# Attention head loop: bias and mask added by identity matmuls in PSUM, and 1/z folded into the transposes of the probabilities

## What is computed

```python
scores = jnp.einsum('bhqd,bhkd->bhqk', q, k) / math.sqrt(HEAD_DIM)
masked = jnp.where(causal[None, None], scores, NEG)
chunk_max = padded.reshape(b, N_HEADS, s, n_chunks, CHUNK).max(axis=-1)
_, topk_idx = jax.lax.top_k(chunk_max, k_top)            # 8 chunks of 16 keys
allowed = causal & (tok_mask | init_mask | recent_mask)  # first 128, last 128 keys too
attn = jax.nn.softmax(jnp.where(allowed, scores, NEG), axis=-1)
out = jnp.einsum('bhqk,bhkd->bhqd', attn, v)
```

## Time and profile before

| | us |
|---|---|
| runs of the kernel before: median (2 runs, 6246.68 to 6270.27) | 6258.47 |
| profiled execution, device time | 6245.39 |
| its span on the slowest core (core 6) | 6243.7 |
| spans of the other cores | 6157.7 to 6235.6 |
| attention stage on core 6, from 1736 to about 4305 | 2569 |

### The profile page before, as it was taken

One profiled execution on the slowest core, in us unless ns is written; L12 is line 12 of the kernel. 1 busy time (PEld: TensorE's weight loads), 2 busy tenths in 40 slices (PEclk: granted clock), 3 DMA queues, 4 the chain that ended last, 5 costly groups with the idle time before them and its releaser, 6 DMA issues.

```text
span 6243.7 us, 55986 instructions; the slowest of 8 cores (6157.7 to 6243.7 us)
## 1 busy us (share of the span) xinstructions
PE 3077.5 (49%) x14003; PEld 1404.8 (22%) x14240; DVE 2022.3 (32%) x4597; ACT 1060.7 (17%) x2316; POOL 762.6 (12%) x1444
## 2 busy tenths in 40 slices
PE   5657665656612233444455555566777511275300
PEld 2222222222201121222222232333333211132100
DVE  1120002121165555555555454452000132211233
ACT  0000000000012232333333333442000022100011
POOL 3323332323300000000000000000222100121000
PEclk9879988888855555555555555556888855587655
DMA  8879996877800000000000000003777633473333
GB/s 135 123 104 138 134 137 100 121 106 113 119 1 7 7 1 8 1 7 1 7 1 1 8 1 7 1 1 78 169 170 166 145 121 121 118 162 64 83 116 114
DMA packets 408685, 471.05 MB, mean 75 GB/s; under 512 B 168064, under 2 KB 284800, under 8 KB 404032
## 3 DMA queue, kind: packets, MB, share of 16 engines
q0 software_dynamic: 207360, 252.27, 28.1%
q1 hardware_dynamic: 201024, 215.19, 11.0%
...
## 4 chain that ended last, share of the span: by engine, by line
DVE 27%; DMA 22%; PE 21%; issue 13%; ACT 11%; SPq 2%; DVEq 2%; another core or an unknown queue 1%; POOL 1%; ACTq 0%; POOLq 0%; PEldq 0%
DMA wqt<-wqT 6%; PE pw L502 5%; ACT Ebuf L445 5%; PE pq L238 4%; DVE Cm L383 3%; DMA wkvt<-wkT 3%; ACT Ebuf L452 3%; PE pk L160 3%; PE psS L434 3%; DMA wot<-woT 3%; DMA wkvt<-wvT 2%; DVE SBc L387 2%; DVE Cm L394 2%; DVE Pn L463 2%; PE pB L778 2%
## 5 line engine op out<-in xcount | busy, mean ns | idle before, releaser
L238 PE MATMUL pq<-xot,wqt 128*128 128x512 bf16 x2008 | 513.5, 404 | 198.3 <-DMA wqt<-wqT 154.9
L160 PE MATMUL pk<-xbt,wkvt 128*128 128x512 bf16 x2006 | 499.2, 394 | 196.4 <-DMA wkvt<-wkT 78.7
L318 PE MATMUL ptr<-identb,Pn 128*128 128x128 bf16 x2304 | 286.3, 307 | 625.8 <-DVE Pn L463 625.8
L502 PE MATMUL pw<-oft,wot 128*128 128x512 bf16 x2007 | 471.4, 390 | 168.3 <-DMA oft<-oscr 135.8
L493 POOL DMA_DIRECT2D wot<-woT x256 | 135.7, 530 | 3101.0 <-ACTq L97 2610.8
L333 PE MATMUL pso<-PT,Vtm 128*128 128x128 bf16 x2304 | 338.4, 265 | 254.2 <-ACT PT L324 105.7
L370 PE MATMUL psS<-Kfm,Qfm 128*128 128x512 bf16 (+1 forms) x624 | 317.7, 555 | 195.0 <-ACT Ebuf L445 188.5
L324 ACT COPY PT<-ptr 128x1024 bf16<-128x1024 bf16 (+3 forms) x384 | 294.6, 802 | 659.8 <-PE ptr L318 659.8
L318 PEld LDWEIGHTS ptr<-identb,Pn 128*128 128x128 bf16 x2304 | 225.5, 139 | 762.8 <-issue 762.8
L445 ACT ACTIVATE Ebuf<-psS,ngm 128x512 bf16<-128x512 f32 (+2 forms) x512 | 301.2, 588 | 308.9 <-PE psS L434 246.7
L452 ACT ACTIVATE Ebuf<-SBf,ngm 128x384 bf16<-128x384 f32 (+1 forms) x256 | 154.5, 604 | 1024.1 <-DVE SBf L421 1003.4
...
## 6 DMA issues: line engine op xcount, KB each, us to landing
xot<-xoT POOLq DMA_DIRECT2D x256, 256.0 KB, 5.6
oft<-oscr SPq DMA_DIRECT2D x256, 256.0 KB, 4.4
xbt<-xbT POOLq DMA_DIRECT2D x256, 128.0 KB, 5.6
wkvt<-wkT POOLq DMA_DIRECT2D x128, 256.0 KB, 7.2
wkvt<-wvT POOLq DMA_DIRECT2D x128, 256.0 KB, 7.1
wqt<-wqT POOLq DMA_DIRECT2D x256, 128.0 KB, 7.1
wot<-woT POOLq DMA_DIRECT2D x256, 128.0 KB, 4.4
...
```

The lines of the kernel that those rows point to most:

```text
L160: ins = te.matmul(pk[kb][:], wkvt[b][:, kb * 128:(kb + 1) * 128], xbt[b][:], start=(ch == 0), stop=(ch == 31))
L238: ins = te.matmul(pq[ob * 2 + hf][:], wqt[b][:, ob * 128:(ob + 1) * 128], xot[b][:, hf * 512:(hf + 1) * 512], start=(ch == 0), stop=(ch == ...
L318: ins = te.transpose(ptr[j][:, t * 128:(t + 1) * 128], Pn[:, kt * 128:(kt + 1) * 128], identb[:])
L502: ins = te.matmul(pw[blk * 2 + hf][:], wot[b][:, blk * 128:(blk + 1) * 128], oft[b][:, hf * 512:(hf + 1) * 512], start=(ch == 0), stop=(ch ...
```

## The change

Inside the attention stage only:

- The causal bias cneg is no longer added by VectorE: TensorE adds it into psS behind the scores by a matmul of the identity with cneg (one piece, or two where the recent part crosses a bank). VectorE reduces the recent part straight from psS; SBc is gone.
- The bias tqb, now bf16, is added into psS in the same way behind the mask matmuls; SBf is gone. The exponentials of the recent part read psS, in one or two pieces, and free its banks.
- VectorE no longer writes Pn. It copies 1/z to bf16 (rzb), and GpSimd makes of it a 128x128 matrix dgrz with 1/z on the diagonal. The transposes become matmuls of each tile of Ebuf with dgrz, into f32 PSUM, in groups of 4 tiles instead of 8.
- The copy of pso to ou goes from VectorE to ScalarE, ahead of the copy mnT of the next head; at a unit's end ScalarE waits for the store in place of VectorE.

```diff
             def emit_pt_av(st):
...
                 for g in range(ngr):
                     j = g % 2
-                    nt = min(8, ntile - g * 8)
-                    p.w(te, "SV", sv_pn)
+                    nt = min(4, ntile - g * 4)
+                    p.w(te, "SG", sg_dg)
                     gs, gv = trg[j]
                     p.w(te, gs, gv)
                     for t in range(nt):
-                        kt = g * 8 + t
-                        ins = te.transpose(ptr[j][:, t * 128:(t + 1) * 128],
-                                           Pn[:, kt * 128:(kt + 1) * 128], identb[:])
+                        kt = g * 4 + t
+                        ins = te.matmul(ptr[j][:, t * 128:(t + 1) * 128],
+                                        Ebuf[:, kt * 128:(kt + 1) * 128], dgrz[hp][:],
+                                        start=True, stop=True)
...
             def emit_oevac(st):
...
-                p.w(vec, "ST", t_av)
-                p.w(vec, "SV")
-                sv_oevac = p.inc(vec.tensor_copy(ou[:, h * 128:(h + 1) * 128], pso[:]), "SV")
+                p.w(sc, "ST", t_av)
+                p.w(sc, "SS")
+                ss_oevac = p.inc(sc.copy(ou[:, h * 128:(h + 1) * 128], pso[:]), "SS")
...
-                    ts = ts_sl[-1]
+                    off = nmid
+                    while off < Nk:
+                        n = min(512 - (base + off) % 512, Nk - off)
+                        p.w(te, "ST")
+                        ins = te.matmul(psS[:, base + off: base + off + n], identb[:],
+                                        cnegB[:, i * 384 + (off - nmid): i * 384 + (off - nmid) + n],
+                                        start=False, stop=True, skip_group_check=True)
+                        off += n
+                    ts = p.inc(ins, "ST")
...
-                    p.inc(vec.tensor_add(SBc[:, 0:W], psS[:, base + nmid: base + Nk], cneg[:, 0:W]), "SV")
-                    sv_sbc = p.cnt["SV"]
-                    if nmid % 512 != 0:
-                        bank_free[(base + nmid) // 512] = ("SV", sv_sbc)
-                    for bank in range((base + nmid + 511) // 512, (base + Nk + 511) // 512):
-                        bank_free[bank] = ("SV", sv_sbc)
                     p.w(vec, "SV")
                     p.inc(vec.tensor_reduce(Cm[:, ncmid:nch],
-                                            SBc[:, 0:W].rearrange("p (c k) -> p c k", k=16),
+                                            psS[:, base + nmid: base + Nk].rearrange("p (c k) -> p c k", k=16),
                                             AX.X, ALU.max), "SV")
...
-                    p.inc(vec.scalar_tensor_tensor(SBf[:, 0:W], SBc[:, 0:W], 1.0, tqb[:, 0:W],
-                                                   ALU.mult, ALU.add), "SV")
...
+                    p.w(te, "SV", sv_tqb)
+                    p.w(te, "SV", sv_cmb)
+                    off = nmid
+                    while off < Nk:
+                        n = min(512 - (base + off) % 512, Nk - off)
+                        p.w(te, "ST")
+                        ins = te.matmul(psS[:, base + off: base + off + n], identb[:],
+                                        tqb[:, off - nmid: off - nmid + n],
+                                        start=False, stop=True, skip_group_check=True)
+                        off += n
+                    t_mask = p.inc(ins, "ST")
...
-                    p.inc(sc.activation(Ebuf[:, nmid:Nk], SBf[:, 0:W], AF.Exp, bias=ngm[:, 0:1],
-                                        accum_out=zparts[:, zcol:zcol + 1]), "SS")
-                    zcol += 1
+                    off = nmid
+                    while off < Nk:
+                        n = min(512 - (base + off) % 512, Nk - off)
+                        p.w(sc, "SS")
+                        ssv = p.inc(sc.activation(Ebuf[:, off:off + n], psS[:, base + off: base + off + n],
+                                                  AF.Exp, bias=ngm[:, 0:1],
+                                                  accum_out=zparts[:, zcol:zcol + 1]), "SS")
+                        zcol += 1
+                        bank_free[(base + off) // 512] = ("SS", ssv)
+                        off += n
...
-                    p.inc(vec.tensor_scalar(Pn[:, 0:Nk], Ebuf[:, 0:Nk], rz[:, 0:1], None, ALU.mult), "SV")
-                    sv_pn = p.cnt["SV"]
-                    pend = (i, h, ntile, sv_pn, kvh)
+                    p.w(vec, "ST", dg_guard[hp])
+                    p.w(vec, "SV")
+                    sv_rzb = p.inc(vec.tensor_copy(rzb[hp][:], rz[:]), "SV")
+                    p.w(gp, "SV", sv_rzb)
+                    p.w(gp, "SG")
+                    sg_dg = p.inc(gp.affine_select(out=dgrz[hp][:],
+                                                   in_=rzb[hp][:, 0:1].to_broadcast([128, 128]),
+                                                   pattern=[[-1, 128]], compare_op=ALU.is_equal,
+                                                   fill=0.0, base=0, channel_multiplier=1), "SG")
+                    pend = (i, h, ntile, ss_exp, sg_dg, kvh, hp)
...
-                p.w(sync, "SV")
+                p.w(sync, "SS")
                 p.w(sync, "QD")
...
-                p.w(vec, "QD")
+                p.w(sc, "QD")
```

More of the change, by code:

```diff
@@ L272, in build @@
         Ebuf = sb2("Ebuf", [128, 2048], BF16)
-        Pn = sb2("Pn", [128, 2048], BF16)
         PT = sb2("PT", [128, 2048], BF16)
-        SBc = sb2("SBc", [128, 384], F32)
-        SBf = sb2("SBf", [128, 384], F32)
         Cm = sb2("Cm", [128, 128], F32)
@@ L283, in build @@
         mnT = sb2("mnT", [128, 128], BF16)
-        tqb = sb2("tqb", [128, 384], F32)
+        tqb = sb2("tqb", [128, 384], BF16)
         zparts = sb2("zparts", [128, 8], F32)
@@ L287, in build @@
         rz = sb2("rz", [128, 1], F32)
+        rzb = [sb2(f"rzb{j}", [128, 1], BF16) for j in range(2)]
+        dgrz = [sb2(f"dgrz{j}", [128, 128], BF16) for j in range(2)]
         ou = sb2("ou", [128, NH * 128], BF16)
@@ L292, in build @@
             psS = sp.enter_context(nc.psum_tensor("psS", [128, 2048], F32))
-            ptr = [sp.enter_context(nc.psum_tensor(f"ptr{j}", [128, 1024], BF16)) for j in range(2)]
+            ptr = [sp.enter_context(nc.psum_tensor(f"ptr{j}", [128, 512], F32)) for j in range(2)]
             ptrM = sp.enter_context(nc.psum_tensor("ptrM", [128, 128], BF16))
@@ L297, in build @@
             trg = {0: ("SV", 0), 1: ("SV", 0)}
+            dg_guard = {0: 0, 1: 0}
             mnT_g = ("SV", 0)
@@ L300, in build @@
             pend_o = None
-            sv_oevac = 0
+            ss_oevac = 0
             t_av_prev = 0
@@ L306, in emit_pt_av @@
                 nonlocal t_av_prev, t_pt_last
-                (i, h, ntile, sv_pn, kvh) = st
-                ngr = (ntile + 7) // 8
+                (i, h, ntile, ss_exp, sg_dg, kvh, hp) = st
+                ngr = (ntile + 3) // 4
                 ev = {}
@@ L323, in emit_pt_av @@
                         p.w(sc, "ST", t_av_prev)
-                    ev[g] = p.inc(sc.copy(PT[:, g * 1024: g * 1024 + nt * 128],
+                    ev[g] = p.inc(sc.copy(PT[:, g * 512: g * 512 + nt * 128],
                                           ptr[j][:, 0:nt * 128]), "SS")
@@ L327, in emit_pt_av @@
                 t_pt_last = p.cnt["ST"]
+                dg_guard[hp] = t_pt_last
                 for kt in range(ntile):
-                    p.w(te, "SS", ev[kt // 8])
+                    p.w(te, "SS", ev[kt // 4])
                     if kt == 0:
-                        p.w(te, "SV", sv_oevac)
+                        p.w(te, "SS", ss_oevac)
                     vsl = Vtm[:, kt * 1024 + kvh * 128: kt * 1024 + (kvh + 1) * 128]
@@ L384, in build @@
                     p.w(vec, "ST", ts)
-                    cneg = cnegB[:, i * 384: i * 384 + W]
-                    p.w(vec, "SV")
-                    p.inc(vec.tensor_add(SBc[:, 0:W], psS[:, base + nmid: base + Nk], cneg[:, 0:W]), "SV")
-                    sv_sbc = p.cnt["SV"]
-                    if nmid % 512 != 0:
-                        bank_free[(base + nmid) // 512] = ("SV", sv_sbc)
-                    for bank in range((base + nmid + 511) // 512, (base + Nk + 511) // 512):
-                        bank_free[bank] = ("SV", sv_sbc)
                     p.w(vec, "SV")
                     p.inc(vec.tensor_reduce(Cm[:, ncmid:nch],
-                                            SBc[:, 0:W].rearrange("p (c k) -> p c k", k=16),
+                                            psS[:, base + nmid: base + Nk].rearrange("p (c k) -> p c k", k=16),
                                             AX.X, ALU.max), "SV")
+                    sv_cmb = p.cnt["SV"]
                     p.w(vec, "SV")
@@ L417, in build @@
                     p.w(vec, "SV")
-                    p.inc(vec.tensor_tensor(tqb[:, 0:W].rearrange("p (c k) -> p c k", k=16),
-                                            fx3, mnbb, ALU.max), "SV")
-                    p.w(vec, "SV")
```

(5 more changed lines are left out.)

10 lines of the change are left out of this document (3 added, 7 removed).

## The result

The changed kernel takes 6164.75 us (median of 11 runs, 6135.5 to 6196.93), the kernel before 6238.14 us beside it (10 runs, 6217.55 to 6298.92): ratio 0.9874, 95% interval 0.9837 to 0.9911, so 1.3% faster. That is about 79 us by the ratio, 73 by the two medians and 78 by the attention stage of the profiles. Forecast were 6215 and a gain of 35 us. The time lies in the range and in the case "within 2%"; the gain is more than double.

A forecast was written before the change was run, and what follows sets the result against it. The prediction held that two nearly equal paths of waits between heads bound the attention stage, with no engine full. Heads -29, GpSimd +23 and unit ends -29 gave -35 us on 6245; forecast 6215, range 6150 to 6290.

The forecast's parts named there:

- within 2%: Outcome case: the changed kernel's time lies within 2% of the kernel before, given a 72% chance.
- E to maxima: From a head's last sum read (E) to the next maxima: -0.13 to -0.33 us in units 0 to 3, -0.20 to +0.06 after.
- tqb matmul: Matmul behind the mask matmuls, on the path: wait 0.15 plus 0.48, +0.63 us a head, +0.65 in two pieces.
- terms per head: Per-head changes in units 0 to 7 without GpSimd's excess, summing to -0.91, times 32 heads = -29 us.
- What would show it: Listed signs: right if heads take 5.0, 8.9, 10.4, 13.5 us in units 0, 3, 4, 7; also signs for each rival.
- I take 0.5, near the second row: GpSimd's time for dgrz, guessed near its 0.530 us DMA issue; excess 0.73 us, times 32 = +23 us.
- Y: GpSimd's time to make dgrz for a head; taken as 0.5 us, with 1.5 held possible.
- meeting points: GpSimd times where its path equals VectorE's: 0.31, 0.46, 0.50, 0.60, 0.60, 0.23, 0.27 us in units 1 to 7.
- The first rival: Slower: the path through GpSimd decides, first transpose waiting for dgrz; 6428 us at a GpSimd time of 1.5; chance 20%.
- 7 x -4.2 = -29 us: At unit ends ScalarE waits for the store while VectorE runs the next head's maxima up to mnegb, saving 29 us.
- The clock rival: Faster: TensorE's clock rises above 0.50 in the heads of units 4 to 7, -137 us, 6075; chance 8%.
- The third rival: Faster: TensorE's waits for itself cost nothing, so tqb and cneg matmuls cost 0.32 us; -108 us, 6105; chance 6%.

The follow-up runs named there:

- e4: Kernel before with only the diagonal matrix through GpSimd (rzb, dgrz, matmuls of Ebuf in groups of 4); ratio 0.9785 to the kernel before.
- e12: Kernel before with only the two bias parts (cneg and tqb added by TensorE in psS); ratio 1.0078 to the kernel before.
- e5: Changed kernel without TensorE's waits for its own last matmul ahead of the cneg and tqb matmuls; ratio 0.974 to the kernel before.
- e6: Changed kernel with GpSimd making the diagonal matrix twice, first into a spare tile; one time, 6273.95 us.
- e11: Changed kernel with plain transposes of Ebuf in place of matmuls with dgrz, division by z left out; one time, 6201.16 us.
- e1: Changed kernel with the copy to ou and the wait for the store back on VectorE; ratio 0.9942 to the kernel before.
- e2: Kernel before with only the copy to ou and the wait for the store moved to ScalarE; ratio 0.9911 to the kernel before.
- e3: Changed kernel with Pn on VectorE and transposes in groups of 8 again, no diagonal matrix or GpSimd; ratio 0.9973 to the kernel before.
- e8: Kernel before with the diagonal matrix and ScalarE's copy to ou and store wait, without the bias parts; ratio 0.9786 to the kernel before.

## Why the prediction was right or wrong

**The reading of the bound was right.** VectorE lost 428 us of work in the heads (1318.13 to 890.45) and the heads gained 41. Where VectorE work gave a gain (Pn, e4) it stood on the path; SBc did too, but what took its place (E to maxima, tqb matmul) gave the gain back (e12).

**The terms per head were right to about 0.1 us.** For units 0 to 7, without GpSimd: forecast -0.93, -0.22, +0.14, -0.36, +0.33, +0.03, +0.20, -0.10; measured medians -0.90, -0.34, +0.07, -0.46, +0.31, -0.03, +0.21, -0.16. The same sum gives -0.91 forecast and -1.30 measured: every unit from 1 to 5 and unit 7 came out 0.02 to 0.12 lower, 12 us over 32 heads. By term: the wait and matmul for tqb 0.15 + 0.48 forecast, 0.62 measured (e5); E to the maxima in unit 7 1.55 forecast, 1.53 measured. "What would show it" named 5.0, 8.9, 10.4 and 13.5 for units 0, 3, 4, 7; it is 5.04, 8.80, 10.37 and 13.17.

**The step that failed first: "I take 0.5, near the second row".** L480, by the view of its line (ns: min, median, max):

```profile
L480 POOL TENSOR_SCALAR_AFFINE_SELECT dgrz<-rzb x256: 287/292/293, 1735.6 to 4213.2; 128x128 bf16<-128x128 bf16 x128
...
  PE ptr L318: 333.5, 254
```

Y was 0.292, below most meeting points (0.31 to 0.60, and 0.23 and 0.27 in units 6 and 7). At Y = 0.29 the same working gives 0.08 x 32 = 3 us in place of +23, and the whole sum -55. Nothing of this term is seen: mnT starts 0.61 us behind the end of mnegb (medians) in every unit from 1 on, before and after, so the path through GpSimd decides nowhere. The row chosen, a DMA issue, was no neighbour of a tile operation. The Trainium skill, GPSIMD Engine Reference, section 3.1, had given an estimate of 0.11 to 0.28 us and some 0.1 more; the trace agrees, with 0.292. The meeting points themselves were right in kind: e6 made the path through GpSimd decide in units 1 to 3, 6 and 7 and hardly in 4 and 5. Single ones were 0.1 to 0.2 us off (e6 above).

**The first rival (GpSimd decides) did not come,** for the same number. But it was near: by e6 the room was below 0.1 us in units 1, 2, 3 and 6, and 0.42 us more cost 61 us, 0.34 to 0.41 a head in these four units.

**Unit ends: "7 x -4.2 = -29 us" was right.** The passages fell by 37, which looks like more. But they are measured from top-8 step to top-8 step, and the wait for the store has not vanished: ScalarE reaches the mask copy mnT of a unit's first head with it still open, and this head is longer for it (by 2.4, 2.0, 1.4, 0.8, 0.4, 0 and 0 us in units 1 to 7, against the unit's median). So 7 us come back inside the heads, and the net is -30. The idle time of line L429 (us and times):

```profile
  DMA oscr<-ou: 32.4, 5
```

against 46.1 in 7 places. In units 6 and 7 the mask comes later than the store, which is then hidden whole.

**The clock rival was partly true.** It had 8% and all of units 4 to 7; it came in a part of unit 7: 11 of 31 heads (7 to 12 by core) at about 12.3 us, the others at 13.17 with the clock at 0.50. 31 heads at 13.17 would be 408 us, the stretch is 400.0. Its mechanism, matmuls in place of transposes, fell with e11. The Trainium skill, TensorE: Matmul & The Clock Gate, Part 4, holds that transposes do not count as busy; by that rule e11 would have lost the rise (0.57 there, 0.56 in after), so e11 speaks against it as the earlier trace rows did. What does bring the rise can be narrowed from all runs. Every kernel with groups of 4 tiles of Ebuf behind GpSimd's short step has it in unit 7 (0.53 to 0.57 on the slowest core: after, e1, e4 to e11); every kernel with Pn in groups of 8 has 0.50 (before, e2, e3, e12). The added matmuls are not it: e4, which has none of them, rises, in the stretch

```profile
3800.00:4150.00 350.00, 217.63 (x1149) 113.22 (x1148) 170.00 (x421) 165.80 (x421) 8.18 (x28) 0.55 0.00 1
```

and e12, which has them all, does not. Nor is it the shorter head: in e6 a head at the clock of 0.50 takes 13.37 us, as long as before, and some rise all the same. Which property of the groups of 4 does it is open.

**The third rival (added matmuls stream) named the right lever.** With the waits, no; without them e5 gives -96, where it had priced -108 (its 0.3 x 11 x 32 is 106).

**The balance.** Diagonal matrix -105 (e4), ou and store -35 (e2), together -143 (e8); the bias parts take 65 back: -78. The prediction summed them in one line per head and so did not see that one half of the change worked against the other.

Of the 43 us between the forecast -35 and the measured -78 about 23 lie in GpSimd's term, 12 in the other terms of the heads, 8 in the clock of unit 7 and 1 at the unit ends. The terms missed in the same direction. The time lies in the forecast's range all the same, since that range, 6150 to 6290, is several times the gain; the size of the gain was missed.

Besides the 108, two sums of the prediction do not come out as written. 6210 and the 13 us to the median are 6223 and not 6215. Y = 0.75 gives 2.28 x 32 - 23 = +50 us and not +60. The 13 us themselves came from two runs (6258.47); with ten the median is 6238.14, 7 us below the profiled execution.
